# A gated attention and feed-forward stack on one core: the row maximum joins the transposed scores through spare partitions, GpSimd splits q and k, and normalising stands one tile behind its statistics

## The reference, cut to what matters

```
x = x + tanh(g_xattn[0]) * attention_L0(layernorm(x), ctx, mask)      # 16 heads of 8, mask [32,128,128]
x = x + tanh(g_ffn[0])   * fp8_linear(layernorm(x))
x = x + tanh(g_xattn[1]) * attention_L1(layernorm(x), ctx)            # causal mask, output projection
x = x + tanh(g_ffn[1])   * mixture_of_8_experts(layernorm(x))         # top 2
x = x + tanh(g_xattn[2]) * per_token_head_attention(layernorm(x), ctx)
x = x + tanh(g_ffn[2])   * quantised_mlp(layernorm(x))
x = x + tanh(g_xattn[3]) * attention_L3(layernorm(x), ctx, mask)      # output projection
x = x + tanh(g_ffn[3])   * mixture_of_8_experts(layernorm(x))

attention: q = xn Wq + bq, k = ctx Wk + bk, v = ctx Wv + bv           # 16 heads, 8 columns each
           p = softmax(mask(q k^T / sqrt(8)));  out = p v  (then Wo, bo in L1 and L3)
```

## Time and profile before

| | us |
|---|---|
| median of the runs | 1914.92 |
| span of the profiled execution | 1906.2 |
| median less that span | 8.7 |
| PE busy | 1579.4 (83%), 12360 matmuls |
| PEld busy | 997.5 (52%) |
| DVE busy | 1396.8 (73%) |
| ACT busy | 684.9 (36%) |
| POOL busy | 521.0 (27%) |
| L866, L868, L873 (transposed scores: mask, q k, maximum), PE busy | 149.4, 152.1, 151.7 |

### The profile page before, as it was taken

How to read it: one execution, slowest core, us unless ns; L and a number is a source line. 1 busy time by engine, 2 the same in 40 slices (tenths; PEclk the granted TensorE clock), 3 DMA queues, 4 the chain that set the end, 5 groups by cost and what they waited for, 6 DMA issues and landing times. The chain is left out here.

```text
span 1906.2 us, 36266 instructions
## 1 busy us (share of the span) xinstructions
PE 1579.4 (83%) x12360; PEld 997.5 (52%) x12360; DVE 1396.8 (73%) x3603; ACT 684.9 (36%) x1218; POOL 521.0 (27%) x565
## 2 busy tenths in 40 slices
PE   3889895388999899889889899935699899787787
PEld 1556563156666556555455555522466666444454
DVE  5777776666676446887888888876567666599997
ACT  1344443134444322333333433412344444333332
POOL 2000000000000002453543453553000000478786
PEclk9999997589999899999999999965999999899998
DMA  6453540244335000000000000004052432000000
GB/s 145 63 72 46 74 59 1 34 134 65 54 53 68 3 1 1 6 1 7 1 6 6 0 7 17 1 0 72 11 68 41 65 52 35 1 1 12 11 12 12
DMA packets 62745, 62.68 MB, mean 33 GB/s; under 512 B 6032, under 2 KB 57744, under 8 KB 62096
## 3 DMA queue, kind: packets, MB, share of 16 engines
q1 hardware_dynamic: 62608, 60.94, 20.1%
HBM read 21.07 MB, written 2.10 MB: 12 GB/s over the span
## 5 line engine op out<-in xcount | busy, mean ns | idle before, releaser
L662 ACT ACTIVATE probs<-bank 128x512 f32<-128x512 f32 x384 | 229.4, 598 | 357.8 <-PE bank L873 351.5
L1220 DVE TENSOR_REDUCE neg_max<-bank 128x4 f32<-128x512 f32 x384 | 260.1, 687 | 123.1 <-PE bank L847 117.5
L1020 PEld LDWEIGHTS bank<-room,area 128*128 128x128 f32 x2048 | 249.3, 195 | 102.7 <-issue 62.5
L447 POOL TENSOR_SCALAR rstd_a<-meanvar 128x4 f32<-128x4 f32 x64 | 17.0, 265 | 1042.9 <-DVE meanvar L1176 1042.9
L1020 PE MATMUL bank<-room,area 128*128 128x128 f32 x2048 | 259.5, 281 | 33.5 <-DVE area L1501 19.0
L737 ACT ACTIVATE work<-bank 128x512 f32<-128x512 f32 (+1 forms) x192 | 114.6, 597 | 356.2 <-PE bank L1045 351.2
L1049 PE MATMUL bank<-xT,room 128*128 128x512 f32 (+1 forms) x384 | 200.5, 604 | 15.5 <-DVE area L1501 15.3
L845 PE MATMUL bank<-mask_b,ident_b 128*128 128x512 bf16 x384 | 153.4, 399 | 62.7 <-DVE neg_max L1220 50.4
L1045 PE MATMUL bank<-xT,room 128*128 128x512 f32 (+1 forms) x384 | 199.2, 601 | 0.0
L1501 DVE TENSOR_TENSOR area<-work,bank 128x512 f32<-128x512 f32 (+1 forms) x192 | 128.7, 679 | 95.7 <-PE bank L1049 75.8
L559 POOL TENSOR_TENSOR prod<-mask_i,work 128x128 f32<-128x128 f32 (+3 forms) x128 | 126.5, 1021 | 155.1 <-DVE mask_i L1562 155.1
(11 more groups left out here) (172 smaller groups left out, 2499.8 us busy)
## 6 DMA issues: line engine op xcount, KB each, us to landing
q_rows<-area SPq DMA_DIRECT2D x144, 128.0 KB
k_rows<-area SPq DMA_DIRECT2D x288, 64.0 KB
ctxT<-ctx_t SPq DMA_DIRECT2D x24, 256.0 KB, 8.4
mask_i<-mask SPq DMA_DIRECT2D x8, 256.0 KB, 8.4
work<-ctx_in SPq DMA_DIRECT2D x8, 256.0 KB, 2.8
out<-x SPq DMA_DIRECT2D x4, 512.0 KB, 3.2
room<-w_down SPq DMA_DIRECT2D x1, 1536.0 KB, 13.7
room<-w_gate SPq DMA_DIRECT2D x1, 1408.0 KB, 6.2
```

What stands on the lines that cost most here:

```text
L662: act.activation(probs[j].rearrange("p a b -> p (a b)"), T_BANK[j % 2][:], ACT.Exp).then_inc(exp_done, 1)
L1020: mm = pe.matmul(dst[:, t * P:(t + 1) * P], h[:, t * P:(t + 1) * P], w, start=i == 0, stop=i == len(terms) - 1)
L1220: dve.tensor_reduce(neg_max[:, 4 * j:4 * j + 4], S_BANK[j % 2][:].rearrange("p (h k) -> p h k", h=4), AX.X, ALU.max, negate=True).then_inc ...
```

## The change

It has four parts.

1. **The maximum rides on unused partitions.** `MAX_ROWS` are partitions 96 to 127 of `q_rows` and `k_rows`. A constant selection matrix, made on the host, is loaded there in both `k_rows` buffers (2 DMAs of 512 KB, `pick_in`). `take_max` writes the transposed maximum there in `q_rows`, in two halves of 32x512 in the place of one copy of 32x128. The four matmuls of L873 go. `scores` uses partitions 0 to 95 only. `turn_max` moves ahead of `weigh(n-1, 2)` and `weigh(n-1, 3)`.
2. **POOL splits q and k.** `split` leaves DVE, and all five instructions of it stand on POOL, with a wait and a `nop` before them. In the middle of an attention POOL starts it after `inv_std`, for group gr+2 in group gr. The first two splits of the attentions stand in POOL's queue too: `split(0, 2)` between `products(last + 3)` and `weighted(last + 2)` of the feed-forward step before.
3. **Normalising one tile later.** `norm` moves from t = 0 to t = 1, `turn_xn` and `take_xnT` from t = 1 to t = 2, `project` q from the middle to the end of t = 2, `project` k and `take_k` from the end of t = 2 to the middle of t = 3 (`take_k` after `exp(n, 1)`), `project` v to the end of t = 3. In attention 0 the statistics for the next step move from t = 2 to 1 and their `normed` from 3 to 2.
4. **Setting up.** POOL no longer makes `pick_max`, `neg_max_t` and the zeros of `q_rows`; DVE clears partitions 0 to 95 of `k_rows` only.

```diff
+SCORE_ROWS = slice(0, 2 * DH * len(Q_SLOTS))
+MAX_ROWS = slice(P - 2 * H, P)
@@ SP
                     if a == 0:
                         load_mask(0, 0)
+                        for buf in range(2):
+                            sp.dma_start(k_rows[buf][MAX_ROWS, :, :, :].bitcast(I32), pick_in).then_inc(pick_loaded, 16)
                         load_rest()
@@ POOL
+            def split(p, a):
+                pool.wait_ge(prep_read, 4 * (G0[a] + p) + 3)
+                if positive(REP * (G0[a] + p)):
+                    pool.wait_ge(rows_spread, REP * (G0[a] + p))
+                for part in range(2):
+                    src = qk if part == 0 else qk_rest
+                    waits_apart(pool)
+                    pool.tensor_copy(parts[:, :, part, :], src).then_inc(pool_steps, ch.one())
+                    pool.wait_ge(pool_steps, ch.count)
+                    pool.tensor_tensor(qk_rest, src, parts[:, :, part, :], ALU.subtract).then_inc(pool_steps, ch.one())
+                    pool.wait_ge(pool_steps, ch.count)
+                waits_apart(pool)
+                pool.tensor_copy(parts[:, :, 2, :], qk_rest).then_inc(split_ready, 1)
@@ POOL, attention(a)
+                split(1, a)
                     for gr, b, _, left in groups(gp, first, last):
                         if left >= 2:
                             inv_std(L0[a] + gr + 3)
+                            split(gr + 2, a)
@@ POOL, feed_forward2
                 products(last + 3, 3, 1)
+                split(0, 2)
                 weighted(last + 2, 2, 1)
@@ ACT, take_max and the body
-                    act.activation(neg_max_t[t % 2][0:2 * H, :], N_BANK[0:2 * H, 0:64].bitcast(BF16),
+                    turned = N_BANK[MAX_ROWS, 0:64].bitcast(BF16).unsqueeze(1).to_broadcast([2 * H, HP // 2, P])
+                    act.activation(q_rows[b][MAX_ROWS, half * HP // 2:(half + 1) * HP // 2, t * P:(t + 1) * P], turned,
                                    ACT.Copy).then_inc(maxT_ready, 1)
-                            take_max(n, t)
+                            take_max(n, b, t, 0)
                             if has_prev:
                                 take_heads(n - 1)
                             exp(n, 0)
+                            take_max(n, b, t, 1)
                             exp(n, 1)
                             if left >= 2 and t == 2:
-                                take_q(gr + 2)
+                                take_xnT(gr + 2)
+                            if left >= 2 and t == 3:
+                                take_k(gr + 2)
                             exp(n, 2)
...
@@ PE, scores_t and the body
+                    if j % 2 == 0:
+                        pe.wait_ge(maxT_ready, 2 * (N0[a] + n) + j // 2 + 1)
                     for i in range(4):
-                        pe.matmul(dst[:, i * P:(i + 1) * P], k_rows[b][:, i % 2, 2 * j + i // 2, tok],
-                                  q_rows[b][:, 2 * j + i // 2, tok], start=False, stop=False)
-                    if j == 0:
-                        pe.wait_ge(maxT_ready, N0[a] + n + 1)
-                    for i in range(4):
-                        mm = pe.matmul(dst[:, i * P:(i + 1) * P], pick_max[:, 4 * j + i, :], neg_max_t[t % 2][:],
-                                       start=False, stop=i == 3)
+                        mm = pe.matmul(dst[:, i * P:(i + 1) * P], k_rows[b][:, i % 2, 2 * j + i // 2, tok],
+                                       q_rows[b][:, 2 * j + i // 2, tok], start=False, stop=i == 3)
@@
                                 scores(n + 1, nb, nt, 0)
+                            turn_max(n)
                             if has_prev:
                                 weigh(n - 1, pb, pt, 2, 0)
                                 weigh(n - 1, pb, pt, 3, 0)
-                            turn_max(n)
...
                             if left >= 2 and t == 3:
-                                project(gr + 2, b, 3)
+                                project(gr + 2, b, 2)
@@ DVE
-                            if splits:
-                                split(gr + 2, 0)
...
                             if t == 0 and left >= 2:
                                 norm_stats(gr + 2, xc - NT + TG * (gr + 3), x_written if a else x_loaded)
+                            if t == 1 and left >= 2:
                                 dve.wait_ge(prep_filled, 4 * (G0[a] + gr + 1) + 1)
                                 norm(gr + 2, L0[a] + gr + 2 if a or (first and b == 0) else 2 * gr + 1)
```

More of the change, by code:

```diff
@@ L103, in program @@
 def program(nc, x_in, ctx_in, ctx_t, mask0, mask3, w_attn, w_ffn0, w_router, w_gate, w_up, w_down, w1, w2, gate3,
-            mlp1, mlp2, mlp2_b, cols_in, rows_in, consts_in, out):
+            mlp1, mlp2, mlp2_b, cols_in, rows_in, consts_in, pick_in, out):
     with ExitStack() as ctx:
@@ L431, in _ @@
             ch = Steps()
-            pool.memset(pick_max[:], 0.0).then_inc(pool_steps, ch.one())
             pool.memset(minus_half[:], -0.5).then_inc(init_pool, 1)
[L434 to L441, removed]
             def inv_std(count):
@@ L467, in body @@
                             inv_std(count)
-                walk(pool, body, ch, 4)
+                        if not last:
+                            split(gp + b + 2, 0)
+                walk(pool, body, ch, 12)
             def attention(a):
+                split(1, a)
                 def body(gp, first, last, a=a):
@@ L537, in feed_forward0 @@
                 inv_std(18)
+                split(0, 1)
             def products(n, t, b):
@@ L699, in body @@
                             exp(n, 3)
-                            if left >= 2 and t == 1:
-                                take_xnT(gr + 2)
                             if left >= 2 and t == 2:
-                                take_k(gr + 2)
+                                take_q(gr + 2)
                 walk(act, body)
@@ L846, in scores @@
                     for i in range(2):
-                        mm = pe.matmul(dst[:, 256 * i:256 * i + 256], q_rows[b][:, 2 * j + i, tok],
-                                       k_rows[b][:, :, 2 * j + i, tok], start=False, stop=i == 1)
+                        mm = pe.matmul(dst[:, 256 * i:256 * i + 256], q_rows[b][SCORE_ROWS, 2 * j + i, tok],
+                                       k_rows[b][SCORE_ROWS, :, 2 * j + i, tok], start=False, stop=i == 1)
                     mm.then_inc(s_filled, 1)
@@ L964, in body @@
                             scores_t(n, b, t, 3)
-                            if left >= 2 and t == 1:
-                                turn_xn(gr + 2)
                             if left >= 2 and t == 2:
-                                project(gr + 2, b, 2)
+                                project(gr + 2, b, 1)
+                            if left >= 2 and t == 3:
+                                project(gr + 2, b, 3)
                             if has_prev and a > 0:
@@ L1281, in attention @@
                         take_mask(0, 0)
-                    for part in range(3):
-                        split(0, part)
                     if a == 0:
@@ L1301, in attention @@
                 split_max(0)
-                for part in range(3):
-                    split(1, part)
                 def body(gp, first, last, a=a, xc=xc):
@@ L1314, in body @@
                                     take_mask(gr + 1, 1 - b)
-                            splits = left >= 2 and t == 3
                             if has_next:
                                 head_max(n + 1, 0)
-                            if splits:
-                                split(gr + 2, 0)
                             if has_next:
@@ L1706, in laid_out @@
         mlp2_b[32 * t:32 * t + E, t] = i["L3_ffn_mlp2_b"]
+    pick = np.zeros((2, H, 2, HP, GT // 2), np.int32)
+    for h in range(H):
+        pick[:, h, h % 2, h // 2] = 0x3F803F80
+    pick = pick.reshape(2 * H, 2, HP, GT // 2)
     c = np.ascontiguousarray
@@ L1716, in laid_out @@
         "mlp2_b": mlp2_b, "cols_in": cols, "rows_in": rows, "consts_in": consts,
+        "pick_in": pick,
     }
```

53 lines of the change are left out of this document (16 added, 37 removed).

## The result

The changed kernel takes 1932.66 us (median; 1929.99 to 1943.82), the kernel before beside it 1914.33: ratio 1.011, interval 1.008 to 1.014. The forecast was 1939 with a range of 1892 to 1990. The profiled execution's span grew from 1906.2 to 1931.8 us, its mean granted clock fell from 0.933 to 0.912.

A forecast was written before the change was run, and what follows sets the result against it. PE's queue was taken to set the pace before, a closed chain through POOL's split and the spread after; +45 in 18 periods and -21 outside, on span 1906.2 plus 8.7 to the median, gave 1939 us (1892 to 1990).

The forecast's parts named there:

- the 18 periods: Group periods from t = 3 of group 0 to group 6 in three attentions: 33.3 to 35.8 us each, +45 us.
- rival 1: The scores, take_k, split, spread chain is there but short: period 33.0, total 1889 us; 24%.
- A closed chain arises: Scores at t = 3, take_k, split, spread, next group's scores: a loop of 35.8 us that sets the period.
- A floor of 33.6: DVE held up beside POOL by up to 5 us a group, making 33.6 us, hidden under the chain's 35.8.
- The starts of attentions 1 and 2: Stretches up to t = 3 lose DVE's split of group 1, early normalising and L873: -7 and -8 us.
- The start of attention 0: POOL splits group 1 only after spread 0 has landed, so little is gained: -1 us.
- The tails: Last five tiles of each attention, each 0.9 us shorter: -12 us in all.
- The start-up and the fp8 step: POOL's clearing gone, its split longer, DVE held up by POOL's split in the fp8 step: together +3 us.
- POOL's queue ahead of attention 2: At the token attention's end, weighted products start late behind split(0, 2), delaying DVE's combining: +4 us.
- Rival 2: The spread does not bind and PE alone sets the period, 28.4 us a group: 1806 us; 5%.
- Rival 3: DVE's memory-port waits before turn_max decide: period 37, 1960 us; 8%.
- Rival 4: POOL's casting copy costs as much as its subtraction: split 13.8, period 39.8 at 12.9, 2011 us; 9%.

The follow-up runs named there:

- e9: Changed kernel with the six DMAs of k's second half left out, every PE, DVE, ACT and POOL instruction kept: 1819.7 us, 0.952 of the kernel before.
- e4: Kernel before with only the maximum on spare partitions; split and normalising as before: 1882.8 us, 0.984 of the kernel before.
- e1: Changed kernel with the last copy of POOL's split made three times: 1996.4 us, 1.043 of the kernel before.
- e5: As e2, with SP's context load for group g+2 issued ahead of the spread of group g+1: 1818.3 us, 0.948 of the kernel before.
- e2: Changed kernel with k projected first of a group's four products, at the end of t = 1: 2011.2 us, 1.050 of the kernel before.
- e7: Changed kernel without the later normalising; maximum on spare partitions and POOL's split stay: 1890.3 us, 0.986 of the kernel before.
- e8: Changed kernel with the six DMAs of k's second half issued by POOL beside SP's twelve: 1937.0 us, 1.011 of the kernel before.
- e11: Changed kernel with groups 0 and 1 of each attention split on DVE, groups 2 to 7 on POOL: 1922.6 us, 1.005 of the kernel before.
- e3: Changed kernel with the split back on DVE; spare-partition maximum and later normalising stay: 1866.9 us, 0.976 of the kernel before.

## Why the prediction was right, and where not

The sign, the time and the mechanism came out, but that the total came so close, 1932.7 for 1939, is luck: two errors cancel. Inside the 18 periods it forecast +45 and got 18 x 1.37 = +25. Outside it forecast -21 and got +1. The mean period of 34.66 is just under the 34.8 at which the forecast's own range began, and in attentions 1 and 2, at 34.4 and 34.3, it is under the 34.5 that was named as a sign of rival 1, as is POOL's work of 7.8 us.

**Part 1.** "A tile without preparing falls to about 6.0 us": 5.97 and 6.08, right. "With part 1 PE alone would need 27.2 us for a group" failed: 29.1 (e9). The 3.6 us of L873 were taken off as if PE decided in each tile; e4 shows 1.2. I had read from the earlier trace rows that PE is busy 205 of 220 us, which is an average, while the tile t = 3 was DVE's.

**Part 3 and the chain.** "A closed chain arises" is shown from both sides: 2.25 us more in POOL's link gave 2.7 (e1); half of k's transfers (e9) or an earlier k (e5) took the wait away and 5.6 to 6.2 us off the period.

| link | forecast | measured |
|---|---|---|
| scores to take_k | 6.6 (5.8 to 7.2) | 7.2 (5.5 to 8.1) |
| hand-overs and POOL's split | 9.3 | 8.1 (8.0 to 8.2) |
| the spread | 19.9 | 19.3 (16.9 to 20.2) |
| sum | 35.8 | 34.6 |

The price of the casting copy, taken from one row with one input at 1.04, was exact (1.04), the subtraction 2.13 against 2.4, and the gaps 0.4 instead of 1.0. The low clock was counted with 0.8 us and takes 1.6 to 2.6 where it strikes. "PE idles about 7 us": 1.2 to 5.6 in its 17 waits, in part because some of the time goes into matmuls at the low level, and because its own work is more than 27.2. In PE's timeline the tile at t = 3 lasts 8.7 to 11.0 us instead of 8.3.

**DVE beside POOL.** "A floor of 33.6" failed by 4.5 us. The losses exist, as the durations of three lines show (ns, min/median/max; in the kernel before, L1242 is the first of them, at most 175):

```profile
L1239 DVE CAST neg_max_parts<-neg_max x96: 174/174/2056, 51.7 to 1648.0; 128x16 bf16<-128x16 f32 x96
```
```profile
L451 POOL CAST area<-area x48: 1037/1037/1337, 19.2 to 1599.5; 128x1024 bf16<-128x1024 f32 x48
L453 POOL TENSOR_TENSOR area<-area x48: 2119/2128/2535, 20.3 to 1600.6; 128x1024 f32<-128x1024 f32 x48
```

But in a group only one `split_max` and one residual add fall beside the split: 1.78 - 0.17 and 0.66 - 0.29 make 2.0 us, not 5. I had taken the 65% of the earlier trace rows, where four instructions of DVE stand against four of POOL, for a mix in which the maxima from the bank (0.69 us with and without POOL) are not slowed at all.

**Outside the periods**, term by term, measured as differences of `turn_max` starts as in the earlier trace rows. The starts of attentions 1 and 2: forecast -7 and -8, measured -7.4 and -8.0. The start of attention 0: -1, measured +2.7. Its first two spreads and POOL's two splits follow one another, and in the second split POOL stands still between the first cast, over at 48.31, and the subtraction behind it:

```profile
55.27 2.12 POOL L453 TENSOR_TENSOR area<-area 128x1024 f32<-128x1024 f32 x1 [6.97 <-issue]
```

So this split lasts 14.7 us and not 7.8, and PE idles 8.3 us before the scores that are first to need its result. The same gap, 6.7 to 7.5 us, stands there in e1, e2, e5, e7, e8 and e9; the profile shows nothing that POOL waited for, so its cause is open.

The tails: -12, measured -2.3. The last wait's tile runs at the low clock (7.96 us in attention 1), and only three tiles with 0.6 to 0.8 each are left between the points; the fifth tile is in the next stretch. The start-up and the fp8 step: +3, measured +1.3 and +5.1. POOL's queue ahead of attention 2: +4, measured +5.75. The end of the kernel, from the last `turn_max` on, took +3.6; across the kernels of the table this stretch lies between 277.6 and 283.4 us, so this may be scatter of single executions, but no run separates it.

The two that I priced low have one cause in common, the split of group 1 beside DVE work on the path. The timeline of DVE and POOL in front of attention 2 shows it:

```profile
1375.04 1.04 POOL L451 CAST area<-area 128x1024 bf16<-128x1024 f32 x1
...
1375.18 4.41 DVE L1206 TENSOR_SCALAR xn<-x,meanvar,rstd 128x128 f32<-128x128 f32 x4 [1.62 <-POOL rstd L441]
```

The normalising of 1.11 us takes 4.41. In the same way the first four steps of the last quantising, 1.8 us in the kernel before, take 6.9 beside `split(1, 1)`; two of them:

```profile
393.25 2.35 DVE L1342 TENSOR_SCALAR work<-room,s 128x512 f32<-128x512 f32 x1
...
396.81 2.23 DVE L1346 TENSOR_SCALAR work<-work 128x512 int32<-128x512 int32 x1
```

In e11, which takes POOL's split out of these places, the stretches ahead of attentions 1 and 2 are 4.6 and 4.8 us shorter. Their starts, with DVE's split of group 1 again, take 5.4 of that back, and the start of attention 0, where POOL's gap is gone too, gives the most: its first t = 3 comes 8.2 us earlier.

**The rivals.** Rival 1 (short chain, 33.0) had POOL's link right at 7.9, but the clock went against it. Rival 2 did not come, yet e5 shows that its period of 28.4 was there to be had by moving k's product and its load. Rival 3: `turn_max` waits for `neg_max_parts` 30.2 us in all (7.9 before the change) against 76.8 for the DMA, so it doesn't decide. Rival 4 is excluded by L451, at 1.04 us.

**What is not settled:** why a spread takes 17 us in some periods and 20 in others, why POOL stands still for 7 us in the second split of attention 0, and why e1's longer split cost some 15 us outside the periods.

## What to carry over

When a step is moved past a wait, draw the loop that it closes, from that wait through every engine and queue back to it, and compare its length with the period; here a split of 8 us was free in one tile and cost 3.1 us a group, against DVE's, in the next. Then look for the link that depends on least (k needs no normalising) and move that one, with its load: e2 and e5 differ by two lines in SP's queue and by 193 us. Savings on an engine that is busy 93% of the time are to be counted tile by tile, since each tile may have another bound.

## What the runs showed of the hardware

- A loop with a wait in it can pay twice: behind an idle time of 0.35 us (e3) the granted clock was 1.00 over the next 5.5 us, behind one of 3.5 us (changed kernel) 0.64 over the next 8.1, for the same instructions.
- DVE's casts, scalar-operand instructions and additions from memory were held up beside POOL (a 128x16 cast from 174 to 2056 ns, the normalising from 1.11 to 4.41 us, the residual add from 0.29 to 0.66), its maxima from the bank were not (0.69).
- Dividing twelve DMAs of 64 KB with 8 destination partitions over two queues did not shorten them: 19.7 us.
